# Four stacked attention layers: the norms' inverse roots computed by GpSimd's power, their rows by VectorE beside the MLPs, and the first norm of the second attention block placed ahead of its weights

## The reference, cut to what matters

```python
x = L0(x, ctx)                  # attention with a residual
x = L1(ctx, x, mask)            # attention, out projection, rmsnorm, MLP (gelu), residual
x = L2(x, ctx, ctx)             # LN, attention, residual; LN, attention, residual; LN, MLP, residual
x = L3(x, ctx, masks)           # LN, self-attention; LN, cross-attention; LN, MLP; each with a residual

def rmsnorm(x, w):
    var = jnp.mean(jnp.square(x), axis=-1, keepdims=True)
    return x * jax.lax.rsqrt(var + EPS) * w
def layernorm(x, scale, bias):
    m = jnp.mean(x, axis=-1, keepdims=True)
    v = jnp.mean(jnp.square(x - m), axis=-1, keepdims=True)
    return (x - m) * jax.lax.rsqrt(v + EPS) * scale + bias
```

## Time and profile before

| what | value |
|---|---|
| median of 3 runs | 2298.61 us (2294.14 to 2299.34) |
| the profiled execution's own time | 2292.91 us |
| its span | 2291.2 us |
| mean granted TensorE clock | 0.955 |
| TensorE busy | 2064.6 us, 90% |
| VectorE, ScalarE, GpSimd busy | 946.5, 1000.0, 656.4 us |

### The profile page before, as it was taken

How to read it: one execution, slowest core, us unless ns; L and a number is a source line. 1 busy time by engine, 2 the same in 40 slices (tenths; PEclk the granted TensorE clock), 3 DMA queues, 4 the chain that set the end, 5 groups by cost and what they waited for, 6 DMA issues and landing times.

```text
span 2291.2 us, 37962 instructions
## 1 busy us (share of the span) xinstructions
PE 2064.6 (90%) x15565; PEld 1638.6 (72%) x15565; DVE 946.5 (41%) x1758; ACT 1000.0 (44%) x2605; POOL 656.4 (29%) x768
## 2 busy tenths in 40 slices
PE   7878788896899999999899999999988987878799
PEld 4555566664788888888788888888855666666566
DVE  3443223204444444445444444443311177776510
ACT  3322444453343443434343344434344367666622
POOL 2311202104132231413224132221121067666500
PEclk9977898998999999999999999999999989999999
DMA  4000000001000000000001000000020010000000
GB/s 136 10 6 2 6 1 1 1 1 42 28 19 19 10 29 1 28 1 19 1 19 47 1 29 10 10 1 1 1 84 1 16 32 1 6 1 6 2 19 19
DMA packets 28174, 38.36 MB, mean 17 GB/s; under 512 B 1744, under 2 KB 19808, under 8 KB 28000
## 3 DMA queue, kind: packets, MB, share of 16 engines
q1 hardware_dynamic: 28000, 35.93, 4.9%
HBM read 33.83 MB, written 2.10 MB: 16 GB/s over the span
## 4 chain that ended last, share of the span: by engine, by line
PE 78%; ACT 8%; DVE 7%; issue 3%; POOL 3%; DMA 1%; SPq 0%; DVEq 0%; ACTq 0%; POOLq 0%
PE ps L184 34%; PE ps L2137 5%; PE ps_four L2283 5%; PE ps_four L2303 5%; PE ps_four L2121 4%; PE ps L2121 3%; PE ps_four L2292 2%; ACT l_pt L1502 2%; PE ps_four L2051 2%; PE ps L2179 2%; POOL l_sm L1352 1%; PE ps L2110 1%; PE ps L2089 1%; PE ps L2097 1%; PE ps L2313 1%
## 5 line engine op out<-in xcount | busy, mean ns | idle before, releaser
L1596 ACT ACTIVATE l_prob<-ps_four,l_mx 128x129 f32<-128x129 f32 x512 | 181.4, 367 | 593.9 <-DVE l_mx L1896 593.9
L1386 POOL TENSOR_TENSOR l_prob<-l_prob,l_mx 128x516 f32<-128x516 f32 x128 | 134.1, 1048 | 782.8 <-DVE l_mx L1903 782.8
L184 PEld LDWEIGHTS ps<-l_wo,l_ao 128*128 128x128 f32 x1536 | 198.8, 190 | 20.8 <-DVE l_ao L1915 6.8
L184 PE MATMUL ps<-l_wo,l_ao 128*128 128x256 f32 x1536 | 206.0, 283 | 5.5 <-DVE l_ao L1915 5.5
L184 PE MATMUL ps<-ctxT,l_wk 128*128 128x512 f32 x768 | 210.3, 409 | 0.0
L184 PE MATMUL ps<-l_hT,l_wq 128*128 128x512 f32 x768 | 210.1, 409 | 0.0
L184 PE MATMUL ps<-l_wv,ctxT 128*128 128x512 f32 x768 | 202.9, 400 | 0.3
L1352 POOL TENSOR_TENSOR l_sm<-l_sm,l_mask 128x1024 f32<-128x1024 f32 x64 | 150.2, 2368 | 132.6 <-DVE l_sm L1861 132.4
L184 PEld LDWEIGHTS ps<-l_wv,ctxT 128*128 128x128 f32 x768 | 142.6, 189 | 42.9 <-ACT l_qT L1577 8.3
L1825 DVE TENSOR_TENSOR x_tok<-x_tok,ps 128x512 f32<-128x512 f32 x98 | 63.5, 684 | 237.2 <-PE ps L2137 177.0
L184 PEld LDWEIGHTS ps<-ctxT,l_wk 128*128 128x128 f32 x768 | 135.7, 190 | 23.1
(11 more groups left out here) (232 smaller groups left out, 3830.8 us busy)
## 6 DMA issues: line engine op xcount, KB each, us to landing
l_staging<-in_L_xattn_wv SPq DMA_DIRECT2D x8, 512.0 KB, 3.6
l_staging<-in_L_xattn_wk SPq DMA_DIRECT2D x8, 512.0 KB, 3.7
l_staging<-in_L_xattn_wq SPq DMA_DIRECT2D x8, 512.0 KB, 4.1
l_staging<-in_L_xattn_wo SPq DMA_DIRECT2D x8, 512.0 KB, 3.8
x_tok<-in_x SPq DMA_DIRECT2D x4, 512.0 KB, 7.5
ctx_tok<-in_ctx SPq DMA_DIRECT2D x4, 512.0 KB, 5.9
l_mlp_w<-in_L_xattn_mlp_w SPq DMA_DIRECT2D x2, 1024.0 KB, 8.7
l_w<-in_L_xattn_w_fc SPq DMA_DIRECT2D x2, 1024.0 KB, 6.5
```

The lines of the kernel that those rows point to most:

```text
L184: ins = e.matmul(out, a, b, start=start and i == 0, stop=stop and i == 2, skip_group_check=not check)
L1386: e.tensor_tensor(pr[:, :, 0:S + 1], pr[:, :, 0:S + 1], mx[:, 3, :].unsqueeze(2).to_broadcast([P, GB, S + 1]), ALU.mult).then_inc(sem("poo ...
L1596: ins = e.activation(pr.t[:, b, 0:S + 1], banks[b // 2].t[:, (b % 2) * (S + 2):(b % 2) * (S + 2) + S + 1], ACT.Exp, bias=mx[:, 1, b:b + 1] ...
```

## The change

The inverse root moves from ScalarE to GpSimd as one power with -0.5; VectorE adds eps before it. GpSimd's stage waits for that sum and for the rows of the norm before on the same tiles. In the stage of layer 2's MLP and in the last stage the rows are VectorE's (no `norm_shift` there). At the start of layer 2's attention, five steps of layer 1's last norm and of the first norm of layer 2 are planned alternately, and then that norm's steps alternately with those of the weights.

```diff
+def alternate(first, other):
+    for _ in first:
+        yield next(other, None)
+    yield from other
...
-        interleave(until_norm(self.l1_last), chain(load_weights(0, 0), normalise(0, 0)), 2.5)
+        first, weights = normalise(0, 0), load_weights(0, 0)
+        for _ in range(5):
+            next(self.l1_last)
+            next(first)
+        interleave(until_norm(self.l1_last), alternate(first, weights), 2.5)
...
+        self.xn_stage = "dve.norm_xn"
         run(norm2(0))
...
         run(mlp2(3))
         pl.emit("l3_mlp_loads", after=("pe.mlp_down", ("l2m", G - 1), FC - 1))
+        self.xn_stage = "act.norm_xa"
...
         run(rest)
+        self.xn_stage = "dve.norm_xn"
         pl.emit("four_given", "l3", emptied=[(self.four_slot.empty, self.four_slot.uses)])
...
+        def norm_rstd(u):                                   # GpSimd
+            nm = self.norms[u]
+            rs = nm["st"]["rs"]
+            q.wait_ge(*pl.done("dve.norm_var", u))
+            if nm["last"] is not None:
+                q.wait_ge(*pl.done(self.norms[nm["last"]]["xn_stage"], nm["last"], 1))
+            e.tensor_tensor(rs[:, 4, :], rs[:, 3, :], self.minus_half[:], ALU.pow).then_inc(sem("pool.norm_rstd"), 1)
...
-        def norm_rstd(u):                                   # ScalarE
-            q.wait_ge(*pl.done("dve.norm_var", u))
...
-            table(ACT.Ln)
-            e.activation(rs[:, 3, :], rs[:, 1, :] if nm["rms"] else mv[:, :, 1], ACT.Ln, bias=self.eps[:, i:i + 1]).then_inc(
-                sem("act.norm_rstd:l"), 1)
-            q.wait_ge(*pl.done("act.norm_rstd:l", u))
-            e.activation(rs[:, 4, :], rs[:, 3, :], ACT.Exp, scale=-0.5).then_inc(sem("act.norm_rstd"), 1)
...
             if not nm["rms"]:
-                ins.then_inc(sem("dve.norm_var"), 1)
+                self.rms += 1
+                q.wait_ge(sem("dve.norm_rms"), self.rms)
+                if nm["last"] is not None:
+                    q.wait_ge(*pl.done("pool.norm_rstd", nm["last"]))
+                e.tensor_scalar(rs[:, 3, :], mv[:, :, 1], nm["eps"], None, ALU.add).then_inc(sem("dve.norm_var"), 1)
                 return
```

More of the change, by code:

```diff
@@ L257, in norm @@
         yield from self.pause()
-        if self.xn_stage == "act.norm_xa" and not rms:
+        stage = self.norms[u]["xn_stage"]
+        if stage == "act.norm_xa" and not rms:
             pl.emit("norm_shift", u)
@@ L262, in norm @@
         for half in range(2):
-            pl.emit(self.xn_stage.split(".")[1], u, half)
+            pl.emit(stage.split(".")[1], u, half)
             yield
@@ L610, in end @@
             h_done = yield from self.norm(t, g, ("ys", g), ("empty", "out32", t, 1), pw, None, True, 1e-6, ("hs", t),
-                                          lambda: pl.free("ys", g, by=(self.xn_stage, t, 1)), split=False)
+                                          lambda: pl.free("ys", g, by=(self.norms[t]["xn_stage"], t, 1)), split=False)
             yield from self.mlp32(t, ("hs", t), h_done, self.plain["mlp_w1"], self.plain["mlp_w2"], b1, ACT.Gelu_apprx_tanh,
@@ L915, in add_bias @@
             def add_bias():
-                self.x_done[g] = self.bias_rows(u, g, self.l3_rows[bias], (self.xn_stage, u, 1),
+                self.x_done[g] = self.bias_rows(u, g, self.l3_rows[bias], (self.norms[u]["xn_stage"], u, 1),
                                                 ("empty", "l3_out_bias", 1))
@@ L1258, in const @@
                             pattern=[[DH, HPT]], channel_multiplier=-1).then_inc(sem("pool.const"), 1)
-            for i in range(2):
-                e.memset(self.eps[:, i:i + 1], (1e-5, 1e-6)[i]).then_inc(sem("pool.const:e"), 1)
+            e.memset(self.minus_half[:], -0.5).then_inc(sem("pool.const:e"), 1)
+            q.wait_ge(sem("pool.const:e"), 1)
             e.memset(self.ones2[:], 0.0).then_inc(sem("pool.const:o"), 1)
@@ L1467, in norm_xa @@
             if half == 0:
[L1468 removed]
+                q.wait_ge(*pl.done("pool.norm_rstd", u))
                 if not nm["rms"]:
@@ L1778, in norm_var @@
             q.wait_ge(sem("dve.norm_rms"), self.rms)
-            e.tensor_tensor(rs[:, 1, :], rs[:, 0, :], mv[:, :, 1], ALU.add).then_inc(sem("dve.norm_var"), 1)
+            if nm["last"] is not None:
+                q.wait_ge(*pl.done("pool.norm_rstd", nm["last"]))
+            e.scalar_tensor_tensor(out=rs[:, 3, :], in0=rs[:, 0, :], scalar=nm["eps"], in1=mv[:, :, 1], op0=ALU.add,
+                                   op1=ALU.add).then_inc(sem("dve.norm_var"), 1)
         def norm_shift(u):
             mv, rs = self.norms[u]["st"]["mv"], self.norms[u]["st"]["rs"]
-            q.wait_ge(*pl.done("act.norm_rstd", u))
+            q.wait_ge(*pl.done("pool.norm_rstd", u))
             e.scalar_tensor_tensor(out=rs[:, 0, :], in0=mv[:, :, 0], scalar=-1.0, in1=rs[:, 4, :], op0=ALU.mult,
```

20 lines of the change are left out of this document (7 added, 13 removed).

## The result

The changed kernel takes 2308.11 us (median of 4 runs, 2307.45 to 2309.05) where the kernel before took 2296.87 (4 runs): a ratio of 1.0054, 95% interval 1.0039 to 1.0069. It is slower by 0.5%. I had forecast 2293.8 with a range that ended at 2302.

What follows compares the result with a forecast made beforehand. TensorE, busy 90% of the span, was taken to bound the kernel. The terms 1.0 - 1.9 - 2.6 - 8.1 + 6.8 summed to -4.8 us, giving 2293.8 us from the median of the runs, range 2283 to 2302.

Steps and rivals of the forecast that it cites:

- What bounds the kernel, and the worth of the table loads: Whole kernel: TensorE bounds it, busy 90%; ScalarE's saved table loads are worth only what stands in TensorE's holes.
- The power, taken at 0.5 us: GpSimd's power in each norm: duration taken as 0.5 us, with 0.2 and 1.5 as ends for the range.
- Layer 1, +1.0: Layer 1's first norm: the power queues behind GpSimd's product, delaying rows and the exponentials TensorE awaits; +1.0 us, bounds 0.7 to 2.
- The start, -1.9: Layer 2's attention start: first matmuls 9.6 us early, then a 5.1 us stop and low clock; net -1.9 us.
- The first softmax, -2.6: Layer 2's first softmax: scores start earlier without ScalarE's wait, a 1.28 us table load enters the path; -2.6 us.
- Layer 2's MLP, -8.1: Layer 2's MLP stage: four holes before transposes vanish, -6.7 us, and 1.4 us of clock return; bounds -5 to -8.1.
- Layer 3's attention, +6.8: Layer 3's attention: two stalls of VectorE +4.2 us, eight added sums +1.3, a table load +1.3; bounds +2 to +12.
- The two norms that I named: Layer 3's attention, group 3's first and group 1's third norm: the power behind both sums delays VectorE's maxima; +2.1 us each.
- The slow power: Rival, chance 0.09: GpSimd's power is slow, seven readers on the path; from 2.2 us the kernel is slower than the bound.
- The cheap relay: Rival, chance 0.32: layer 3's relay absorbs the waits and the power is cheap; +6.8 becomes about +2, whole 2289 us.
- That the start gives nothing: Rival, chance 0.12: loads at layer 2's start take 6 us each, wo's split ends past 554; whole 2297 us.
- That the table loads matter: Rival, chance 0.02: ScalarE is a bound, so 18 loads gone, 23 us, shorten the kernel to 2276 us.

Runs made afterwards that it cites:

- power_cheap: The changed kernel with a product in place of GpSimd's power, so the inverse root is not computed: 2301.57 us, 1.0029 of the kernel before.
- power_twice: The changed kernel with a second power, into a row that nothing reads, ahead of each power: 2313.52 us, 1.0080 of the kernel before.
- placement_alone: The kernel before with only the new order at layer 2's start, roots and rows as before: 2287.40 us, 0.9963 of the kernel before.
- power_alone: The kernel before with the roots by GpSimd's power and nothing else, rows and placement as before: 2317.71 us, 1.0080 of the kernel before.
- rows_alone: The changed kernel with ScalarE's logarithm and exponential in place of VectorE's sum and GpSimd's power: 2284.02 us, 0.9931 of the kernel before.
- root_first_table: As root_first, with the exponential's table loaded right behind layer 2's last gelu: 2302.35 us, 1.0027 of the kernel before.
- root_first_sums: As root_first, with the norms' sums with eps moved from VectorE to GpSimd, ahead of the power: 2303.80 us, 1.0037 of the kernel before.
- root_first: The changed kernel with layer 3's eight powers moved in GpSimd's queue right behind their statistics: 2299.39 us, 1.0024 of the kernel before.
- mlp_stage_alone: The kernel before with power and VectorE's rows only in the six norms of layer 2's MLP stage: 2287.56 us, 0.9965 of the kernel before.

## Why the prediction was wrong, point by point

The terms beside what the profiles of after show against those of before, first against first and second against second:

```
                         forecast   first    second
layers 0 and 1             +1.0      +1.2     +1.4
start of L2                -1.9      +0.4     +0.4
first softmax              -2.6      +0.6     +0.5
L2 attention and tail       0        +7.7     +2.4
L2 MLP                     -8.1      -8.8     -9.2
L3 attention               +6.8     +13.1    +15.7
last stage                  0        +0.3     +0.2
sum                        -4.8     +14.5    +11.4
```

Three steps failed, and together they turn a small gain into a loss. The largest is layer 3's attention, where the waits behind the power and the added sums were priced at half of what the stage lost (6.8 against 13.1 and 15.7). The second is the pair of gains ahead of it, -4.5 us for the start and the first softmax where the runs show +0.9 to +1.0. The third is the clock, put at nothing in layer 2's attention and its tail, where it took 2.4 to 7.7 us.

**What bounds the kernel, and the worth of the table loads: right.** 18 loads (nine of each set) and 49 us of ScalarE's work went, and where TensorE didn't wait for ScalarE nothing came of it.

**The power, taken at 0.5 us: mis-sized, it took 1.02.** The end of 1.5 held it. By power_cheap and power_twice its price is 4.3 us for 0.82 and 7.7 for 1.02, so the error of 0.5 us cost some 3 to 4. The estimate from the Trainium skill (GPSIMD Engine Reference, section Performance versus the Vector engine), 0.33 us, is three times too low: its factor of two is for plain elementwise work, and no row here puts a power there.

**Layer 1, +1.0: the wait right, the match of the stretch luck.** 1.4 us more of wait at that place, in both profiles of after. The 1.2 in layers 0 and 1 together shows nothing: in kernels with ScalarE's root there, the same stretch took 512.2 to 520.8 us.

**The start, -1.9: the mechanism right to the holes, the sum wrong.** Forecast: a hole under 9 us, then one of 5.1. Measured: 9.30 and 5.37. The second norm's transposes came 1.3 us before those of the old kernel, 2.5 with the 1.2 that layer 1 had cost, where I had 4.5. The 2 us are the loads of wk and wq (GpSimd idle 3.81 and 4.55 us for them, where I had 3.7 each), the power's half us, and half a us before the first value matmuls. The clock then took back what was left, and the stretch is 0.4 us longer. It took 4.5 us and not 2.6. I had charged the low stretch behind the new hole alone, but the shorter first hole also puts matmuls into the low stretch around it, which had been spent idle: placement_alone, without the second hole, has 1.7 us more of matmul time there. The larger error was to take the second hole as given. I had the power's 12 us in the queue in my own working, and counted it as the price of the placement. It is the price of the power: with ScalarE's root the same placement is worth 8.2 us, and the power without the placement costs 7.

**The first softmax, -2.6: the table load right, the comparison and the end wrong.** The kernel came into this stretch 1.6 us later than before. The scores started 0.6 later and the transposes 0.4 earlier, so 1.0 and 2.0 us were gained up to there, where I had 1.6 and 2.6, the difference being the power's half us. The table load fell in the path as said. But those gains were not GpSimd's. My sum set the new end of GpSimd's product, 585.9, against the old transposes at 588.18, and the old product had ended at 585.05 + 1.16 = 586.21: like against like that is 0.3 us. The 2 us behind it were TensorE's own matmuls at the low clock (the lower level from 579 to 586 us), which the profile of after runs faster there (0.87 granted over this stretch before, 0.94 after). And I stopped at the transposes. Behind them the next scores wait for a copy behind the norm's bias in GpSimd's queue, 2.23 us where it was 0.93, and the gain was gone, 26.3 us against 25.7.

**Layer 2's MLP, -8.1: right.** 8.8 and 9.2 us shorter in the two profiles, all four holes gone, no table load left in the stage. The reason was half of it: VectorE's rows aren't needed for it, since either part alone does it (power_alone 127.3, rows_alone 128.4).

**Layer 3's attention, +6.8: the mechanism right, the size off by 6.3 us in the first profile and 8.9 in the second.** The two norms that I named are the two that stall VectorE most, by 4.62 and 4.70 us. In the one shown, the maxima start at 1940.38, 3.9 us behind the first sum's end (1934.10 + 2.34 = 1936.44), where I had 3.0: half a us more is the power's, half a us the norm's own `norm_shift` (0.68 us, where I had 0.16). The subtraction behind them then gave back the 0.9 that I had said, so by my way of counting these two norms cost 6.0 us and not 4.2. "In the other six [...] nothing waits" was wrong by three waits of 0.48 us. The table load cost 1.5 us in its place, where I had 1.3 (2.24 us of wait at the next scores where the kernel before had 0.77). The eight added sums took 6.0 us of VectorE in the first profile and 8.0 in the second, where I had 1.3, up to 2.4 us beside GpSimd's sums. The Trainium skill (SBUF — State Buffer, section Who interferes with whom) says that a `tensor_scalar` in a two-port mode and GpSimd block each other for a whole instruction, and that a VectorE instruction with two inputs in that memory contends with a GpSimd instruction that reads it. The trace agrees: 1.93 and 1.40 us for instructions that take 0.17 and 0.16 alone.

What failed is thus the size of two terms: the stall (3.0 us each, with nothing in the other six) and the sums (0.16 us each, though my own row of L1785 had a longest of 1.41). What the runs show in their place: 4.4 to 6.9 us of the stage go when the powers are moved ahead of the sums with the mask. With them moved the stage is still 8.7 us longer than before. The table load, 1.4 us, and VectorE's sums are what the rows show to be left of the change there, but taking out the one gave nothing (root_first_table) and moving the other 2 us (root_first_sums), so how the 8.7 us divide is open. Adding up stalls of VectorE, as if the relay passed each on one for one, is not shown to be right. Other orders of the same relay, with ScalarE's roots in it, took 344.4 to 348.7 us, so some 4 of the 8.7 may be nothing but which VectorE instruction meets which of GpSimd's.

**What I had at zero.** Layer 2's attention and its tail are 3.8 and 3.9 us longer in the first pair of profiles and 2.4 and 0.0 in the second, with TensorE's idle time the same to 0.2 us in the attention. That is the clock. My range made no room for it, and it is as large as most of my terms.

**The rivals.** The slow power was the nearest, with chance 0.09: it ended on the right side, at 1.02 us and not at its 2.2, since the queue took more than the seven places' own time. The cheap relay, 0.32, fell: the stage lost 13.1 us and not 2, and with fewer waits in root_first it was shorter. That the start gives nothing, 0.12, came true in the number and not in its reason: the loads took 3.8 and 4.5 us, not 6, and the last split ended at 551.6 us, not past 554. That the table loads matter, 0.02, fell.

## What to carry to other kernels

An instruction moved to another engine costs its place in that engine's queue as well as its duration, and here mostly the place: a power of 1.02 us stood 12 us in the queue. Ask what stands ahead of it there at the moment it is wanted, and what on the reading engine stands behind the wait. A change of parts should be priced part by part and place by place, also where the parts come together. Here one was worth 8 us until another took it back, and using the power in six norms in place of 28, with ScalarE's root in the others, turned +0.5% into -0.8%. A saving on an engine that isn't waited for is worth nothing even at 49 us.

## What the runs showed of the hardware that I had not expected

GpSimd's power costs 0.82 us more than a product on the same 128x4 (1.02 against 0.20).

TensorE's clock fell to its lower level, 1.2 of 2.4 GHz, behind a stretch at 6.3 of 10 us busy in one kernel (mlp_stage_alone) and not in another that did the same there (the kernel before). Over layer 2's attention the clock made 2.2 to 4.6 us between kernels in which TensorE had the same matmuls and was idle within 0.3 us as long, and 4.1 us in the tail between two profiles of one kernel. The whole changed less, 2305.7 and 2304.2 us, since other stretches went the other way. A term of that size in a single profile is not a result; the median over rounds is.

A hole can hide a low stretch. In the kernel before, 5.4 us of matmuls at the start of layer 2 ran at the lower level, and in the changed one, with 4.1 us less of holes, 13.8 us did.
